# A cross-attention and sign-FFN block on one core: another order of work for the first three requests

## The reference: what is computed

```python
xn = layernorm(x)                                  # over the 256 features
q = xn @ W.T + b
logits = q @ ctx.T + (1 - mask) * -1e9             # 256 x 77 per request
x = x + tanh(g_xattn) * softmax(logits) @ ctx
x = x + tanh(g_ffn) * layernorm(x) @ sign(weight).T
```

## Time and profile before

| | |
|---|---|
| runs | 289.94 us median of 3 (288.92, 289.94, 296.21) |
| profiled execution | 289.57 us, of which the profile's span is 287.8 us |
| busy, share of the span | PE 276.7 us (96%), PEld 266.1 (92%), DVE 247.7 (86%), ACT 247.2 (86%), POOL 214.7 (75%) |
| chain that ended last | PE 92%, no other engine over 2% |
| DMA | 49.15 MB, mean 171 GB/s |
| granted clock of PE, mean | 0.989 |

### The profile page before, as it was taken

How to read it: one execution, slowest core, us unless ns; L and a number is a source line. 1 busy time by engine, 2 the same in 40 slices (tenths; PEclk the granted TensorE clock), 3 DMA queues, 4 the chain that set the end, 5 groups by cost and what they waited for, 6 DMA issues and landing times.

```text
span 287.8 us, 9285 instructions
## 1 busy us (share of the span) xinstructions
PE 276.7 (96%) x2222; PEld 266.1 (92%) x2222; DVE 247.7 (86%) x814; ACT 247.2 (86%) x709; POOL 214.7 (75%) x585
## 2 busy tenths in 40 slices
PE   6799999999999999999999999999999999999982
PEld 6679999999999999999999999999999999999961
DVE  3488899989989998998989999988999899898882
ACT  1489999999999999999999999999999999999742
POOL 2466877887788778877878887788778877886543
PEclk9799999999999999999999999999999999999997
DMA  7951566666556655556566555556656665541212
GB/s 197 279 143 49 175 212 179 191 186 189 164 174 204 212 179 165 193 184 173 169 212 207 180 170 175 173 186 184 212 175 180 189 188 163 170 154 73 76 65 81
DMA packets 53698, 49.15 MB, mean 171 GB/s; under 512 B 23792, under 2 KB 37168, under 8 KB 53680
## 3 DMA queue, kind: packets, MB, share of 16 engines
q1 hardware_dynamic: 52832, 48.42, 55.3%
q10 hardware_dynamic: 848, 0.53, 0.7%
HBM read 32.15 MB, written 16.78 MB: 170 GB/s over the span
## 4 chain that ended last, share of the span: by engine, by line
PE 92%; ACT 2%; DMA 1%; POOL 1%; issue 1%; DVE 1%; POOLq 0%; SPq 0%; ACTq 0%
PE ffn_ps L709 20%; PE pv_ps L691 18%; PE l_ps L672 17%; PE ctx_ps L604 12%; PE xt_ps L636 10%; PE x1t_ps L678 9%; PE pt_ps L655 5%; DMA ctx_v<-in_ctx_dram 1%; PE ctx_ps L594 1%; POOL y L344 1%; POOL rstd L306 0%; ACT L377 0%; DVE x_lo L559 0%; DVE c L548 0%; ACT ffn_scaled L432 0%
## 5 line engine op out<-in xcount | busy, mean ns | idle before, releaser
L306 POOL TENSOR_TENSOR rstd<-ve,minus_half 128x2 f32<-128x2 f32 x128 | 89.2, 697 | 10.0
L672 PE MATMUL l_ps<-m_sb,x_t 128*128 128x77 f32 x512 | 78.1, 256 | 0.8 <-ACT m_sb L383 0.5
L672 PEld LDWEIGHTS l_ps<-m_sb,x_t 128*128 128x128 f32 x512 | 74.6, 191 | 2.1 <-ACT x_t L408 1.6
L370 ACT ACTIVATE xs<-x_in,shift,rstd 128x256 f32<-128x256 f32 x126 | 74.5, 592 | 0.0
L678 PE MATMUL x1t_ps<-ident,x 128*128 128x128 f32 x256 | 68.8, 273 | 0.0
L691 PE MATMUL pv_ps<-ctx_v,p_t 77*128 77x256 f32 x256 | 66.1, 380 | 0.0
L709 PE MATMUL ffn_ps<-wf_t,x_hi 128*128 128x256 f32 x256 | 56.0, 300 | 2.5 <-DVE x_lo L559 2.4
L559 DVE TENSOR_TENSOR x_lo<-x1t_ps,x_hi 128x512 fp32r<-128x512 f32 x64 | 44.2, 691 | 15.9 <-ACT x_hi L439 15.9
L567 DVE SCALAR_TENSOR_TENSOR x<-pv_ps,c,x_in 128x256 f32<-128x256 f32 x128 | 55.5, 475 | 0.4 <-PE pv_ps L691 0.4
L344 POOL TENSOR_TENSOR y<-ffn_scaled,x 128x256 f32<-128x256 f32 x64 | 46.5, 727 | 9.1 <-ACT ffn_scaled L432 9.1
L467 DVE BATCH_NORM_STATS2 st<-x_in 128x6 f32<-128x512 f32 x64 | 44.8, 702 | 6.2 <-DMA x_in<-in_x_dram 6.2
(11 more groups left out here) (50 smaller groups left out, 431.5 us busy)
## 6 DMA issues: line engine op xcount, KB each, us to landing
x_in<-in_x_dram SPq DMA_DIRECT2D x64, 256.0 KB, 2.8
out_dram<-y SPq DMA_DIRECT2D x64, 256.0 KB, 2.1
ctx_v<-in_ctx_dram SPq DMA_DIRECT2D x32, 154.0 KB
mask_in<-in_mask_BxSxS_ik_dram SPq DMA_DIRECT2D x32, 154.0 KB, 3.5
ctx_sq<-in_ctx_dram SPq DMA_DIRECT2D x116, 40.0 KB, 2.3
wq_raw<-in_L_xattn_W_dram ACTq DMA_DIRECT2D x1, 256.0 KB, 4.2
wf_raw<-in_L_ffn_weight_dram ACTq DMA_DIRECT2D x1, 256.0 KB, 5.3
bq_col<-in_L_xattn_b_dram ACTq DMA_DIRECT2D x1, 1.0 KB, 4.5
```

Source lines behind the costliest of these rows:

```text
L306: pool.tensor_tensor(res[:, i], ve[:, i], minus_half[:], ALU.pow).then_inc(res_done, 1)
L370: act.activation(xs[:, n % 2, j], x_in[:, n % N, j], ACT.Identity, scale=rstd1[:, n % R, j:j + 1], bias=shift1[:, n % R, j:j + 1]).then_in ...
L672: ins = pe.matmul(l_ps[:, j * K:(j + 1) * K], x_t[:, r % 2, c, j * P:(j + 1) * P], m_sb[:, c, r % R], start=(c == 0), stop=(c == C - 1))
```

## The change

Slots 0 and 1 are no longer run by the loop of slots. Each engine has a list of its own for them, and `pipeline` begins at slot 2. In that list:

- ACT issues only the loads of W and its bias, then applies Exp once to two columns, and issues the loads of the FFN weight and the gates behind that. The row sum of one half of W is made by ACT (an accumulating copy), of the other half by DVE.
- The second half of the first projection goes to the bank pt_ps instead of ctx_ps, and follows the first with nothing between.
- The transposes of requests 0 and 1 go to two banks, xt_ps and ffn_ps0. One half is copied by ACT, the other by DVE (`transposed_half`).
- DVE scales the rows of requests 0, 1 and 2 (before: of 0), ACT from request 3 on.
- PE runs the logits of request 0 behind two `warm_up` transposes, then the transposes of request 1, the keys of requests 2 and 3, the logits of request 1. The eight `warm_up` transposes of slot 0 are gone.
- The sum, mean and subtraction for the FFN weight stand behind the residual of request 0 on DVE; its transposes on PE and copies on ACT stand inside slot 2.
- The moments of requests 4 and 5 and the transpose of the keys of requests 4 and 5 stand in front of slot 2 on DVE; POOL has the layer norm of request 4 there.

```diff
-        def pipeline(eng, slot, after={}):
+        def pipeline(eng, slot, begin=0):
...
```

```diff
             act.dma_start(wq_raw[:], wq_rows).then_inc(wq_loaded, DMA)
             act.dma_start(bq_col[:], b_q.rearrange("(p c) -> p c", c=C)).then_inc(bq_loaded, DMA)
+
+            act.wait_ge(half_ready, 3)
+            act.activation(first_exp[:], one[:], ACT.Exp)
             act.dma_start(wf_raw[:], w_ffn.rearrange("(c p) i -> p c i", c=C)).then_inc(wf_loaded, DMA)
             act.dma_start(g_raw[:, 0:1], g_xattn.partition_broadcast(P)).then_inc(gates_loaded, DMA)
             act.dma_start(g_raw[:, 1:2], g_ffn.partition_broadcast(P)).then_inc(gates_loaded, DMA)
 
+            act.wait_ge(wq_loaded, DMA)
+            act.activation(wq_copy[:], wq_raw[:, 1], ACT.Copy,
+                           accum_out=row_sum[:, 1:2]).then_inc(wq_sum_done, 1)
             keys_step(0, 1)
             m_step(0, 0, 1)
+            m_step(1, 0, 2, pt_ps)
...
+            def transposed_half(n):
+
+                act.wait_ge(xt_psum, n + 1)
+                act.activation(x_t[:, n, 0], xt_ps[:, 0], ACT.Copy).then_inc(xt_done, 1)
...
+            transposed_half(0)
+            transposed_half(1)
+            exps(0, 0)
+            act.wait_ge(gates_loaded, 2 * DMA)
+            act.activation(g_tanh[:], g_raw[:], ACT.Tanh).then_inc(tanh_ready, 1)
+            keys_step(1, 2)
+            transposed_p(0, 0)
+            exps(0, 1)
+            m_step(0, 1, 3)
+            transposed_x(0, 2)
+            m_step(1, 1, 4)
             for j in range(T):
-                scale_rows(0, 1, j)
-
-            def gates():
-
-                act.wait_ge(gates_loaded, 2 * DMA)
-                act.activation(g_tanh[:], g_raw[:], ACT.Tanh).then_inc(tanh_ready, 1)
+                scale_rows(0, 3, j)
...
+                if isinstance(t, int) and t == 2:
+                    ffn_weights()
...
+            def stats1_later(n):
+                dve.wait_ge(x_loaded[n], DMA)
+                dve.wait_ge(mr1_done, n - R + 1)
+                moments(x_in, st1, n, n % R, stats1_done)
+
+            def scale_rows(n):
+                dve.wait_ge(shift1_done, n + 1)
+                at_least(dve, xt_psum, n - 1)
+                for j in range(T):
+                    dve.tensor_scalar(xs[:, n % 2, j], x_in[:, n, j], rstd1[:, n, j:j + 1], shift1[:, n, j:j + 1],
+                                      ALU.mult, ALU.add).then_inc(xs_done, 1)
+
+            def transposed_half(n):
+
+                dve.wait_ge(xt_psum, n + 1)
+                dve.tensor_copy(x_t[:, n, 1], ffn_ps[0][:, 0:S]).then_inc(xt_half_done, 1)
+
...
+            stats1(1)
+            scale_rows(0)
+            transposed_half(0)
+            scale_rows(1)
+            stats1(2)
+            logits_there(0)
+            logits(0)
+            transposed_half(1)
+            dve.wait_ge(wf_loaded, DMA)
+            dve.wait_ge(prep_step, prepared(dve.tensor_scalar(wf_neg[:], wf_raw[:], 0.0, None, ALU.is_lt)))
+            signs = prepared(dve.scalar_tensor_tensor(out=wf_sign[:], in0=wf_raw[:], scalar=0.0, in1=wf_neg[:],
+                                                      op0=ALU.is_gt, op1=ALU.subtract))
+            logits_there(1)
+            logits(1)
+            scale_rows(2)
+            stats1(3)
+            dve.wait_ge(tanh_ready, 1)
             for j in range(T):
-                dve.tensor_scalar(xs[:, 0, j], x_in[:, 0, j], rstd1[:, 0, j:j + 1], shift1[:, 0, j:j + 1],
-                                  ALU.mult, ALU.add).then_inc(xs_done, 1)
-            stats1(1)
-            stats1(2)
-
...
+                dve.tensor_copy(gate_attn[:, j:j + 1], g_tanh[:, 0:1])
+                ins = dve.tensor_scalar(gate_ffn[:, j:j + 1], g_tanh[:, 1:2], ROOT, None, ALU.mult)
+                ins.then_inc(gate_ready, 1)
+            prob_recip(0, 0)
+            dve.wait_ge(gate_ready, 2)
+            attn_scale(0, 0)
+            residual1(0, 0)
+            dve.wait_ge(prep_step, signs)
+            dve.wait_ge(prep_step, prepared(dve.tensor_reduce(row_sum[:, C:2 * C], wf_sign[:], AX.X, ALU.add)))
+            dve.wait_ge(prep_step, prepared(dve.tensor_scalar(row_mean[:, C:2 * C], row_sum[:, C:2 * C],
+                                                              1.0 / D, None, ALU.mult)))
+            for c in range(C):
+                ins = dve.tensor_scalar(wf_c[:, c], wf_sign[:, c], row_mean[:, C + c:C + c + 1], None,
+                                        ALU.subtract)
+            ins.then_inc(wf_ready, 1)
+            stats1_later(4)
+            transposed_keys(0, 4)
+            stats1_later(5)
```

And on PE and POOL:

```diff
             m_step(0, 0, 2, 1)
+            m_step(1, 0, 2, 2, pt_ps)
...
-            transpose_x(0, 0)
-            m_step(1, 0, 2, 2)
-
-            def pair_keys(t0, r):
-                pe.wait_ge(ctx_loaded[(r + 2) % N // 2], landed(t0, r + 2))
-                pe.wait_ge(m_done, t0 + r + 2)
-                keys_step((r + 2) % N)
...
+            def transpose_halves(n):
+
+                pe.wait_ge(xs_done, T * (n + 1))
+                for c, half in enumerate((xt_ps[:, 0], ffn_ps[0][:, 0:S])):
+                    for j in range(T):
+                        ins = pe.transpose(half[:, j * P:(j + 1) * P], xs[:, n, j, c * P:(c + 1) * P], ident[:])
+                ins.then_inc(xt_psum, 1)
+
+            def pair_keys(t0, n):
+                pe.wait_ge(ctx_loaded[n % N // 2], landed(t0, n))
+                pe.wait_ge(m_done, t0 + n)
+                keys_step(n % N)
+
+            transpose_halves(0)
+            warm_up(2)
+            pe.wait_ge(xt_done, 1)
+            pe.wait_ge(xt_half_done, 1)
+            pe.wait_ge(m_done, 2)
+            logits(0, 0)
+            transpose_halves(1)
+            pair_keys(0, 2)
+            pe.wait_ge(xt_done, 2)
+            pe.wait_ge(xt_half_done, 2)
+            pe.wait_ge(logits_done, 1)
+            logits(0, 1)
+            transpose_p(0, 0)
+            m_step(0, 1, 4, 3)
+            values(0, 0)
+            transpose_x(0, 2)
+            m_step(1, 1, 4, 4)
...
-                if begins:
-                    warm_up(8)
-                    pair_keys(t0, r)
...
+                if isinstance(t, int) and t == 2:
+                    ffn_weights()
...
             norm1(0)
             norm1(1)
             pool.wait_ge(mask_loaded[0], DMA)
             negmask(0)
+            negmask(1)
             norm1(2)
-
-            def gates():
-                pool.wait_ge(gate_ready, 2)
+            norm1(3)
+            pool.wait_ge(mask_loaded[1], DMA)
+            pool.wait_ge(logits_done, 1)
+            negmask(2)
+            norm1_later(4)
+            pool.wait_ge(gate_ready, 2)
```

More of the change, by code:

```diff
@@ L357, in slot @@
                     negmask(r + 1)
-            pipeline(pool, slot, {1: gates})
+            pipeline(pool, slot, 2)
         @block.scalar
@@ L561, in slot @@
                 if exists(t0, r - 1):
[L562 to L573 removed]
+                    residual1(t0, r - 1)
                 if exists(t0, r + 4):
```

195 lines of the change are left out of this document (102 added, 93 removed).

## The result

| | before | after |
|---|---|---|
| median of 20 runs each | 289.61 us (288.54 to 296.24) | 290.84 us (289.35 to 292.92) |
| ratio after to before | | 1.0047, 95% interval 1.0029 to 1.0065 |
| profiled execution, span | 289.57, 287.8 | 290.15, 288.3 |
| granted clock of PE, mean | 0.989 | 0.999 |

A forecast was written before the change was run, and what follows sets the result against it. PE was taken to bound the kernel, busy 276.7 of 287.8 us. Profiled 289.57 − 1.85 for the earlier FFN of request 0 + 1.4 for a clock fall behind PE's gap gave 289.1 us, range 287.0 to 290.4.

The forecast's parts named there:

- Nothing from slot 3 on is changed: From slot 3 on work stays the same, so the effect is how much earlier the FFN of request 0 starts.
- slots of the same length: Sign: slots after slot 3 keep their length, but for a stretch of clock 0.50 just behind F.
- The start of DVE's chain at 9.97: In the front, DVE's moments of request 2 start at 9.97, set by its x landing; bounds 9.7 and 10.3.
- F: Start of the FFN of request 0 on PE: 23.70 before, 21.85 forecast, gain 1.85 us (1.2 to 2.6).
- the path behind it: From DVE's moments of request 2, through POOL's norm of request 4 and ACT, to F: 11.88 us.
- The half copy: On DVE, a half copy out of PSUM behind the logits of request 0: 0.36 us, bounds 0.33 and 0.44.
- gap and clock: PE idles about 2.0 us before F; the clock falls behind it, 1.4 us lost (1.0 to 1.7); chance 0.53.
- Rival B: Gates landing after 12.75 hold up ACT at the tanh; 290.5 us at a landing of 14.2; chance 0.08.
- The base: The sum starts from the profiled execution of before, 289.57 us; nothing added for the runs' median of 289.94.
- C: x of request 2 lands at 9.7, shorter copies and waits: F near 21.1, 286.9 us; chance 0.05.
- D: ACT's work behind POOL's norm of request 4 keeps F at 23.5: 289.4 us; chance 0.04.
- A: PE's gap before F does not cost the clock: 287.7 us; chance 0.30.

The follow-up runs named there:

- experiment 1: The change with its two new tiles allocated behind all others, so every other tile keeps its address of before: 289.66 us, ratio to before 1.0009.
- experiment 2: The kernel before with two unused tiles of the same sizes added where the change has them: 290.93 us, ratio to before 1.0031.
- Experiment 9: experiment 4 without the two gate loads, gates set to 1.0, so the output is not the reference's: 286.94 us, ratio to before 0.9919.
- experiment 12: experiment 4 with each gate loaded as one value to one partition and spread by a one-row matmul: 286.71 us, ratio to before 0.9914.
- experiment 3: experiment 1 with 18 filler transposes on PE before the FFN of request 0: 289.20 us, ratio to before 0.9996.
- experiment 4: experiment 1 with x_hi and the FFN weight's copies ahead of request 4's scaled tile and request 2's exponentials on ACT: 287.37 us, ratio to before 0.9938.
- experiment 7: experiment 4 with the rows of request 2 scaled by ACT instead of DVE: 287.77 us, ratio to before 0.9958.
- experiment 10: The change, unchanged, profiled a second time: 291.71 us at clock 0.986.
- experiment 11: experiment 4 with eight filler transposes on PE before the FFN of request 0: 287.86 us, ratio to before 0.9962.
- experiment 13: experiment 1 with each gate loaded to one partition and spread by a one-row matmul, ACT's order kept: 289.47 us, ratio to before 1.0011.
- experiment 6: experiment 1 with the load of x of request 2 issued ahead of the first mask load: 290.07 us, ratio to before 1.0025.

## Why the prediction was wrong

**The step that failed first: "Nothing from slot 3 on is changed".** The instructions are the same, their addresses are not. Two new tiles lengthen the FFN's matmuls and every slot, by 0.86 us from slot 3 on in the two profiled executions; experiment 1 takes it away and experiment 2 puts it into before. The prediction had no rival for it. It named only the sign that would show it, slots of the same length.

**The start of DVE's chain at 9.97, bounds 9.7 and 10.3.** It was read from one execution. x of request 2 was ready for DVE at 9.97 there, at 10.68 in the second profile of before, and at 11.17 and 11.08 in the two of the change. Of the gates' loads the prediction asked only whether they land in time for ACT; it didn't ask what 2 × 128 pieces of 4 bytes do to the other loads. Experiment 9 shows that they make the lull from 6.5 to 9 us, experiment 12 that the gates can be had without it. With these loads DVE waited for x of request 2, 0.66 to 1.63 us, in five of the seven profiles of the change's kind that load in its order (after, experiments 1, 3, 4, 7, 10, 11), without them in none of three (experiments 9, 12, 13). The lower bound, 9.7, had a wrong reason too: the FFN weight's load does not start later, it is issued at 1.71, before at 1.65. In before a late landing is covered by DVE's own waiting; the change packs DVE up to 9.73, so each later tenth reaches F. By the same lull the context of requests 2 and 3 is late for a PE that now asks at 10.7, and behind that wait the clock can fall (experiments 6 and 10). This wait was not in the prediction.

**Right: the path behind it.** 11.88 us were worked out from the moments to F; 11.94, 11.94 and 12.05 came (after, experiments 1 and 13). The half copy took 0.42, within its bounds. One small term was missing: an FFN that starts on a standing PE takes 1.19, not 0.92, so of 1.85 at F at most 1.6 reach slot 3. The 0.92 is the chain's: in PE's timeline of before the FFN's first matmul starts at 23.46 already, while the transposes ahead of it are still under way.

**Right in mechanism: gap and clock.** A gap of 2.1 came, and with it a low clock in about half the runs (6 of 12 in experiment 1, 8 of 12 in experiment 13); the profile of experiment 1 shows the fall behind the gap. The fall's price is 1.6 (experiment 1; 1.55 between the two medians of experiment 13), where 1.4 was taken. By the trace of experiment 13, 289.57 − 1.83 + 0.27 = 288.0 without a fall and 289.6 with one, against 287.96 and 289.51 measured. The Trainium skill (TensorE: Matmul & The Clock Gate, "Why this matters for your kernels") wants only gaps of more than about 3 us avoided; the runs here disagree, with falls behind PE waits of 0.8, 1.1, 1.8 and 2.1 us (experiments 3, 6, 10 and 1). With a gap of 1.00 us before F low clocks were rare (2 of 12 in experiment 4, 0 of 7 in experiment 12).

**Rival B's premise.** ACT had no wait at the tanh, but not for the reason given. The prediction let the gates be issued about 1.5 later, behind the table load; the last was issued at 2.66 against 2.65 before, and landed 8.2 us later, at about 10.9 instead of the assumed 11.9.

**The base.** The sum started from one profiled execution with a clock fallen in the front. Runs of before with no low clock take 288.78 in the median, and those of experiment 1 288.29: a gain of 0.5, or of 0.8 with the 287.96 of experiment 13, not 1.85. The second profile of before (289.39, no fall in the front) has F at 23.48, which takes only 0.2 of the difference. I have no profile of before at 288.8, so what F is there stays open.

**Put together.** Against before the change loses about 0.9 us by its tiles (0.6 to 1.0 in the profiles, 0.1 to 1.7 by the runs of experiment 2). Where the clock holds, the late load leaves almost nothing of the path's gain to set against it. And 12 of 20 runs pay 1.3 more for low clocks, where before pays 1.1 in 29 of 90 (289.89 less 288.78). How the low runs of the change divide between the front and the gap isn't known, since only profiled executions show where the clock fell. These parts are not exact to a few tenths: among runs without a low clock the change lies 1.5 above experiment 1, among those with one 0.7. Rivals B, C and D did not come; A did in 8 of 20 runs, without its gain.

## What to carry to other kernels

Before moving an engine's work up against a load, ask how far that load's landing scatters, and what else in the DMA queues moves many tiny pieces at the time: spreading a single value over 128 partitions by a one-row matmul left the DMA engines free here (experiments 12 and 13), though it shortened the kernel only where its front hung on these loads. Allocate new tiles behind the old ones, or measure the shift by itself, before a change of order is judged. When a path is shortened on an engine that then feeds PE, follow PE's new gaps: one of 1 us before F was mostly free here, one of 2 us cost 1.6 us in about half the runs.
